# Layer 0's h made one group ahead of the projections that read it, in a two-layer graph attention kernel

## The reference

```python
# layer 0
h = relu(layernorm(x))
m   = h @ map_w.T + map_b                       # 8 heads of 64
cos = (m / |m|) @ (m / |m|).T  per head, masked ; cos_adj = cos > 0.1
q, k = m @ q_w.T + q_b, m @ k_w.T + k_b
p   = softmax(where(mask, NEG, q @ k.T / 8)) * keep
A   = cos_adj * p
out = relu((A @ (h @ gcn_map_w.T + gcn_map_b)) @ gcn_W.T / (A.sum(-1) + 1))
x = x + out
# layer 1: h = relu(layernorm(x)); 4-head masked attention on h, projected out; x = x + that
```

## Time and profile before

| | |
|---|---|
| median of 3 runs | 2962.06 us (2953.75 to 2968.97) |
| the profiled execution, its own time | 2967.72 us |
| its span, first to last instruction | 2965.3 us |
| TensorE busy | 2723.9 us, 92% of the span |
| VectorE, ScalarE, POOL busy | 2011.9, 1743.9, 1578.7 us |
| mean granted TensorE clock | 0.97 of full speed |
| DMA engines' busy share | queue q1, 56.7% |

### The profile page before, as it was taken

One profiled execution on the slowest core, in us unless ns is written; L12 is line 12 of the kernel. 1 busy time (PEld: TensorE's weight loads), 2 busy tenths in 40 slices (PEclk: granted clock), 3 DMA queues, 4 the chain that ended last, 5 costly groups with the idle time before them and its releaser, 6 DMA issues. The chain is left out here.

```text
span 2965.3 us, 63358 instructions
## 1 busy us (share of the span) xinstructions
PE 2723.9 (92%) x20883; PEld 1479.9 (50%) x20886; DVE 2011.9 (68%) x6356; ACT 1743.9 (59%) x4891; POOL 1578.7 (53%) x4146
## 2 busy tenths in 40 slices
PE   5999999999989999999999999957999999999997
PEld 3444444444544454444444444434556555555554
DVE  4476777676767676777677667656666766676764
ACT  3466666565656565656656566535666666666663
POOL 1466566556655665566556646523554455545541
PEclk8999999999999999999999999968999999999998
DMA  4265655655565656565656556555665656556652
GB/s 126 55 123 122 128 132 123 131 123 129 123 137 123 133 122 128 125 132 124 132 133 125 121 126 138 107 133 119 157 155 146 160 146 158 149 144 159 152 137 64
DMA packets 826070, 385.37 MB, mean 130 GB/s; under 512 B 722832, under 2 KB 724368, under 8 KB 825744
## 3 DMA queue, kind: packets, MB, share of 16 engines
q1 hardware_dynamic: 825744, 381.33, 56.7%
HBM read 146.32 MB, written 67.11 MB: 72 GB/s over the span
## 5 line engine op out<-in xcount | busy, mean ns | idle before, releaser
L510 ACT ACTIVATE probs<-probs,negmax 128x128 f32<-128x128 f32 x1024 | 398.2, 390 | 553.1 <-DVE negmax L119 553.1
L161 PE MATMUL ps_pj<-wm_hi,hT 128*128 128x512 f16 x1024 | 340.4, 395 | 99.9 <-DMA hT<-h 84.4
L427 POOL TENSOR_TENSOR o_sb<-o_sb,xres 128x512 f32<-128x512 f32 x128 | 162.9, 1272 | 460.6 <-DVE o_sb L650 457.3
L119 DVE CUSTOM_DVE_ANT_0 probs<-ps_sc,mask 128x128 f32<-128x128 f32 x1024 | 236.5, 286 | 197.5 <-PE ps_sc L835 196.1
L161 PE MATMUL ps_pj<-wv_hi,hT 128*128 128x512 f16 x1024 | 326.8, 380 | 0.0
L161 PE MATMUL ps_pj<-hT,wq_hi 128*128 128x512 f16 x1024 | 310.4, 385 | 0.0
L161 PE MATMUL ps_pj<-hT,wk_hi 128*128 128x512 f16 x1024 | 305.8, 380 | 0.0
L1103 ACT ACTIVATE l_probs<-l_probs,l_negmax 128x128 f32<-128x128 f32 x512 | 199.1, 390 | 150.2 <-DVE l_negmax L119 150.2
L1072 POOL TENSOR_TENSOR l_xres<-l_xres,l_bo_rows 128x512 f32<-128x512 f32 x128 | 171.0, 1336 | 158.4 <-DMA l_xres<-x_scratch 158.3
L632 DVE SCALAR_TENSOR_TENSOR c<-cprobs,c 128x512 f16<-128x512 f32 x256 | 205.2, 802 | 36.9 <-ACT c L517 28.2
L161 PEld LDWEIGHTS ps_pj<-wm_hi,hT 128*128 128x128 f16 x1024 | 103.0, 101 | 225.8 <-DMA hT<-h 95.2
(11 more groups left out here) (192 smaller groups left out, 7037.6 us busy)
## 6 DMA issues: line engine op xcount, KB each, us to landing
xg<-in_x SPq DMA_DIRECT2D x32, 1024.0 KB, 5.8
xres<-in_x SPq DMA_DIRECT2D x128, 256.0 KB, 2.9
x_scratch<-o_sb SPq DMA_DIRECT2D x128, 256.0 KB, 2.1
xg<-x_scratch SPq DMA_DIRECT2D x128, 256.0 KB, 3.0
l_xres<-x_scratch SPq DMA_DIRECT2D x128, 256.0 KB, 3.4
out<-l_o_sb SPq DMA_DIRECT2D x128, 256.0 KB, 3.7
cpT<-c SPq DMA_TRANSPOSE x256, 3.3
mask_u<-in_adj SPq DMA_DIRECT2D x32, 64.0 KB, 5.7
```

The costliest lines, as they stand in the source:

```text
L119: last = nc.vector.tensor_tensor_reduce(masked[:, i], scores[:, i // 2, (i % 2) * P:(i % 2 + 1) * P], mask, -1.0, FLOAT_MAX, ALU.add, ALU. ...
L161: last = pe.matmul(out, a(kt), b(kt), start=(n == 0), stop=(n == 3 * kts - 1))
L427: nc.gpsimd.tensor_tensor(o_sb[:, j % 2], o_sb[:, j % 2], xres[:, j % 2], ALU.add).then_inc(res_done, 1)
L510: last = nc.scalar.activation(probs[:, i], probs[:, i], ACT.Exp, bias=negmax[:, u % 2, i:i + 1], scale=-1.0, accum_out=zsum[:, u % 4, hh:h ...
```

## The change

h's factors, relu, split and transposes of group t + 2 are made during group(t), one group before the projections read them. In group(t) the order is now: POOL `factors(t+2)` at u = 0; ScalarE `relu` and `h_high` (t+2, u-2) at u = 2 to 5, behind n_high; VectorE `h_low(t+2, u-3)` at u = 3 to 6, ahead of n_low and p_low; SyncE `transpose_h(t+2, u-3)` at u = 3 to 6, between transpose_n and transpose_p. xg is loaded one group further ahead: `load_graphs(t+3)` stands at u = 6 behind transpose_p, and all four `stats(t+3, j)` at u = 7 between row_max and epilogue. `convert_mask` goes from u = 5 to u = 6. In front of the first group all of group 1's h is made and group 2's x is loaded.

```diff
+            def load_graphs(g):
+                sp.wait_ge(relu_done, count(QUAD * g))
+                sp.dma_start(xg[:], xt[g]).then_inc(x_loaded, 16)
...
             for j in range(QUAD):
                 transpose_n(0, j)
-                if j == 2:
-                    transpose_h(1, 0)
+                transpose_h(1, j)
+            load_graphs(2)
...  SyncE, group(t)
                     if proj and 3 <= u < 3 + QUAD:
                         transpose_n(t + 1, u - 3)
-                    hg, hj = (t + 1 + (u + 1) // 8, (u + 1) % 8)
-                    if hj < QUAD and hg < GROUPS:
-                        transpose_h(hg, hj)
+                    if ahead and 3 <= u < 3 + QUAD:
+                        transpose_h(t + 2, u - 3)
                     transpose_p(8 * t + u)
+                    if t + 3 < GROUPS and u == 6:
+                        load_graphs(t + 3)
                     if ahead and u == 1:
-                        sp.wait_ge(relu_done, count(QUAD * (t + 2)))
-                        sp.dma_start(xg[:], xt[t + 2]).then_inc(x_loaded, 16)
                         sp.wait_ge(mask_ready, count(t + 1))
...  POOL, group(t)
-                    if proj and u == 5:
+                    if ahead and u == 0:
+                        factors(t + 2, 0, QUAD)
+                    if proj and u == 6:
                         convert_mask(t + 1)
-                    if ahead and u == 6:
-                        factors(t + 2, 0, QUAD)
...  ScalarE, group(t)
-                    hg, hj = (t + 1 + (u + 2) // 8, (u + 2) % 8)
-                    if hj < QUAD and hg < GROUPS:
-                        relu(hg, hj)
-                        h_high(hg, hj)
+                    if ahead and 2 <= u < 2 + QUAD:
+                        relu(t + 2, u - 2)
+                        h_high(t + 2, u - 2)
...  VectorE, group(t)
-                    hg, hj = (t + 1 + (u + 1) // 8, (u + 1) % 8)
-                    if hj < QUAD and hg < GROUPS:
-                        h_low(hg, hj)
+                    if ahead and 3 <= u < 3 + QUAD:
+                        h_low(t + 2, u - 3)
...
-                    if ahead and u in (4, 5):
-                        stats(t + 2, 2 * (u - 4))
-                        stats(t + 2, 2 * (u - 4) + 1)
+                    if t == 0 and u == 0:
+                        for j in range(QUAD):
+                            stats(2, j)
+                    if t + 3 < GROUPS and u == 7:
+                        for j in range(QUAD):
+                            stats(t + 3, j)
```

More of the change, by code:

```diff
@@ L543, in _ @@
             for b in range(KT):
-                if b >= 2:
-                    relu(1, b - 2)
-                    h_high(1, b - 2)
+                relu(1, b)
+                h_high(1, b)
                 q_copy(0, b)
@@ L552, in group @@
             def group(t):
-                proj = t + 1 < GROUPS
+                proj, ahead = t + 1 < GROUPS, t + 2 < GROUPS
                 for u in range(8):
@@ L731, in _ @@
             for b in range(KT):
-                if b == 2:
-                    h_low(1, 0)
+                h_low(1, b)
                 n_low(0, b)
```

## The result

The changed kernel takes 3031.41 us (median of 4, 3026.8 to 3039.37) against 2958.51 for the kernel before in the same comparison: ratio 1.0244, 95% interval 1.0206 to 1.0283. It is slower, by 73 us; 3016 was forecast, with a range of 2940 to 3055. The profiled execution took 3028.03 us (span 3026.2).

What follows compares the result with a forecast made beforehand. POOL's norms chain through SyncE's store and transposes to cpT(5) was taken to bound the cycle. 57.03 + 1.33 + 1.0 + 1.0 + 0.25 gave 60.6 us a cycle against 58.82, so 3016 us, range 2940 to 3055.

Steps and rivals of the forecast that it cites:

- signs of being wrong: Prediction wrong if xg lands before VectorE gets there, norms are not longer, or TensorE doesn't wait at u=6.
- hT one group early: TensorE's waits for hT at u=0 to 3 go; worth 0.37 us on the chain, leaving 57.03.
- SyncE's order, +1.33: On SyncE, transpose_h ahead of transpose_p at u=5 issues cpT(5) later, adding 1.33 us a cycle.
- h_low beside POOL's norms, +1.0: VectorE's h_low subtractions, moved to u=3 to 6, slow POOL's small norm instructions, adding 1.0 us a cycle.
- net two more: Each step's POOL norms meet net two more VectorE subtractions, 0.4 to 0.5 us each.
- the stated bounds: Limits for h_low's cost to POOL's norms: 0 if subtractions fall into gaps, 1.5 us for three full ones.
- The statistics at u=7, +1.0: VectorE, doing four stats at u=7, waits for xg loaded at u=6; POOL's norms start 1.0 us later.
- Jitter and clock, +0.25: Jittering landings and clock lost after the longer stall at u=6 add 0.25 us a cycle.
- the port: VectorE and POOL lock each other out of SBUF; h_low's move therefore costs POOL's norms 1.0 us a cycle.
- Rival 1: xg's load is in time, so VectorE doesn't stand at u=7: cycle 58.9 us, 2962 us; chance 0.14.
- Rival 2: hT waits are real gain, with h_low under 0.9 us and xg in time: 57.9 us, about 2934; chance 0.18.
- Rival 3: xg lands 1 us later, clock falls, n_high holds ScalarE: cycle 62.2 us, 3061 us; chance 0.10.

Runs made afterwards that it cites:

- experiment 3: Kernel before, with SyncE's store and residual load of a step moved behind its transposes: 2934.84 us, ratio 0.9922.
- experiment 11: Kernel of experiment 10 with xg in quarters, one ahead of each step's transposes at u=3 to 6: 2791.06 us, ratio 0.9429.
- experiment 1: Kernel after, with transpose_h moved behind transpose_p on SyncE: 3047.95 us, ratio 1.0305.
- experiment 2: Kernel after, with xg loaded in four quarters, one behind the transposes of each step u=3 to 6: 2951.55 us, ratio 0.9989.
- experiment 9: Kernel of experiment 8 with transpose_h moved behind transpose_p: 2949.26 us, ratio 0.9966.
- experiment 7: Kernel after, with the whole load of xg ahead of the three transposes of u=6: 2980.93 us, ratio 1.0073.
- experiment 8: Kernel of experiment 2 with each quarter of xg ahead of its step's transposes: 2978.4 us, ratio 1.007.
- experiment 4: Kernel after, with transpose_h behind transpose_p, xg in quarters placed last, and store and residual load behind the transposes: 2876.56 us, ratio 0.9731.
- experiment 5: Kernel after, with xg in quarters behind the transposes and transpose_h behind transpose_p: 2943.62 us, ratio 0.9959.
- experiment 6: Kernel of experiment 4 with each quarter of xg ahead of its step's transposes: 2788.59 us, ratio 0.9428.
- experiment 10: Kernel after, with store and residual load behind the step's three transposes: 2980.75 us, ratio 1.0075.

## Why the prediction was right, point by point

The sign and the size came out, the sign by the mechanism that the prediction said decides it (xg's load at u=6), the size partly by luck: a cost that hardly came and others that came larger cancelled. One of its own signs of being wrong showed: POOL's norms did not get longer.

**hT one group early.** Right: no wait for hT is left, and with SyncE's order as it is here that is no gain in itself. Experiment 3 shows the exchange of the two waits from the other side. It becomes a gain when the store no longer stands ahead of the transposes: without h one group early that kernel takes 2934.84 us (experiment 3), with it and the quarters 2791.06 (experiment 11). The quarters in the kernel of 3 were not run, so how much of the 144 us is h's alone stays open.

**SyncE's order, +1.33.** The size is right: cpT(5) left 3.79 us behind the residual instead of 2.39, +1.40. That it adds to the cycle is not: experiment 1 took it out and nothing came back. In the kernel after it is not what closes the cycle. The waits for cpT were foreseen as 3 to 4 us a cycle at u=6; there they are 2.13, in 25 of 28 cycles, and the total of 3.97 is made up by the 1.83 at u=4, which the prediction had seen and rightly priced at nothing.

**h_low beside POOL's norms, +1.0.** Wrong. POOL's chain took 30.61 us, against 30.5 in clean cycles and a mean of 31.05 before, which had 0.55 us of idle time in it (0.02 after). Where the three subtractions stand back to back on VectorE, three of POOL's small instructions run long; here in the cycle shown, VectorE and then POOL:

```profile
1126.75 0.68 DVE L590 TENSOR_TENSOR h<-h 128x512 f16<-128x512 f32 x1
1127.35 0.69 DVE L612 SCALAR_TENSOR_TENSOR n<-m_sb,n 128x512 f16<-128x512 f32 x1
1128.19 0.73 DVE L633 SCALAR_TENSOR_TENSOR c<-cprobs,c 128x512 f16<-128x512 f32 x1 [0.16 <-ACT c L520]
```

```profile
1126.80 0.69 POOL L77 TENSOR_TENSOR norm_st<-norm_st 128x8 f32<-128x8 f32 x1
1127.57 0.53 POOL L78 TENSOR_TENSOR norm_st<-norm_st,consts 128x8 f32<-128x8 f32 x1
...
1128.45 0.53 POOL L76 TENSOR_TENSOR norm_st<-norm_st 128x8 f32<-128x8 f32 x1
```

Counted between 200 and 1800 us, 218 small instructions of POOL ran long before (8.0 a cycle) and 262 after (10.0). So the "net two more" of the step is right, and its price is not: they lose 0.36 us each over the usual 0.20 instead of 0.43, and the sum of what they lose is nearly the same, 93 us in both, or 3.4 us a cycle before and 3.6 after. The traces also show why three in a row cost less each. Every one of the 218 and 262 long instructions ends 0.05 to 0.10 us, nearly always 0.06, behind the end of such a subtraction (as 1127.49 behind 1127.43 above), and none of the usual length lies inside one: a POOL instruction loses what is left of the subtraction when it comes, not the whole of it. Before, it came 0.13 us after the subtraction's start in the mean, and after, with three in a row, 0.20. The 10 long ones of a chain lost 3.55 us against 3.40 for 8 before: +0.15, near the lower end of the stated bounds. The price is not fixed: in experiments 1, 2 and 9, with h_low in the same place, the 10 lost 3.8 to 3.9 us and the chain took 30.9 to 31.0, so some 0.45. The rule of the Trainium skill (SBUF — State Buffer, section Who interferes with whom), that the port pair shared by VectorE and GpSimd is an exclusive lock, agrees with these ends of instructions; the 1.4 that the prediction worked out from it does not, since it took two whole subtractions where only their remainders are lost.

**The statistics at u=7, +1.0.** The mechanism is right in each of its parts: VectorE's stand of 2.71 us, in all 29 cycles that load xg (2 to 3, some 29 times, were forecast; two more stands lie ahead of them), m_copy late, TensorE held at u=1, POOL late. Its size was +1.49 against before's mean, or +1.68 against 13.64. The term mis-sized is the load: forecast 5.4 us behind the issue of cpT(5) and 5.7 to land, so 14.7 us from the residual to the first statistics; measured 9.38 to the issue and 6.68 from there to use, 16.06. From the end of the statistics to POOL's norm it is 11.12, where the prediction's figures give 14.64 - 3.6 = 11.04. The landing of 1 MB behind six transposes takes 1 us longer, and the issue is 0.2 further behind that of cpT(5) than forecast. Of the excess of 0.68 over the forecast 14.64, 0.4 is xg's arrival against u0 (u0 + 0.93 instead of 0.55; u0 is later too), 0.24 the statistics (3.29 instead of 3.05), and the rest what follows them. The 14.64 is near the median of 14.73; the mean is drawn up by the 8 late cycles. The prediction's 4.9 us for this load, an estimate by the Trainium skill (DMA: Bandwidth & Descriptors, Specifications and the anatomy of one DMA), lies below every landing after as well (5.7 at the least); the fixed cost in it is one that the page gives for DMAs issued from GpSimd, and these are issued by SyncE.

**Jitter and clock, +0.25.** Too small. Taken with the rest of the cycle, from the matmul of cpT(5) to the next u0 it is 7.80 in the mean, against 7.18 + 0.25, and 8.70 in the cycle shown, where TensorE has just stood 2.95 us. That stretch, with the columns of the earlier trace rows:

```profile
1155.50:1164.20 8.70, 8.69 (x68) 4.30 (x69) 3.35 (x14) 3.15 (x11) 1.26 (x1) 0.80 0.97 244
```

TensorE is busy throughout at a clock of 0.80, the mix of 2.4 and 1.2 GHz of the earlier trace rows. Over the 1600 us the mean clock fell from 0.99 to 0.97.

**The sum.** Against the forecast of 60.61 the terms are +0.68 (to the norms), -0.94 (POOL), +0.17 (SyncE), +0.15 (landing), +0.37 (rest): 61.04. The port's 0.94 too much was outweighed by 1.37 too little in the other four. 0.43 a cycle in 29 cycles is 12 us; the profiled execution came 6 us over the 3022 that were named for it, and the median 15 over 3016. What the prediction did not see is that it had written down two loops and added their terms. It closed the cycle with cpT(5) and let xg's delay enter as a term; in fact xg's arrival hangs on the same POOL chain through nearly three transposes more, and runs in a loop of its own:

```
2nd residual to xg's issue          9.38
issue to first statistics           6.68
four statistics                     3.29
to POOL's first norm               11.12
POOL's chain                       30.61
                                   61.08
```

Both sums give the cycle, as any walk round it does, and stands do not tell them apart: VectorE stands for xg in every cycle, but TensorE stands for cpT(3) in every cycle too, and for cpT(5) in 25 of 28. The experiments that change one loop each decide it: shortening the way to cpT(5) gains nothing (1), shortening the arrival of xg gives back 80 us (2). Without the stand POOL starts some 12.8 us after u0 (experiments 7 to 9), and the loop through cpT(5) sums to about 58.5 us, no longer than the 58.84 of before. So the sign came from xg's loop alone: with xg in time the change is worth nothing either way (experiment 2). The advice drawn from the sum (put transpose_h behind transpose_p) would have been wrong for the kernel after.

**The rivals.** Rival 1 (xg in time, 58.9 us, 2962 us): the chip has it in experiment 2, 58.77 us and 2951.55 us. Its price was right, though with 1.0 for the port where 0.45 was paid; its condition does not hold in the change. Rival 2 (57.9 us, 2934 us) had its first condition met, the port costing under 0.9, but not its second. Experiment 2 meets both and still takes 58.77, so its price was 0.9 us a cycle too low. Rival 3 (everything late, 3061 us) had in it the late landing of xg behind six transposes and more clock loss, and 3031 lies between it and the forecast.

## What to carry to other kernels

Where a cycle has several loops of nearly one length through one in-order queue, write down each loop with its sum before pricing a move: the term of a loop that doesn't close the cycle is worth nothing. A stand of an engine in every cycle makes a loop a candidate and no more, since here two engines stood in every cycle; an experiment that shortens one loop alone decides. On an in-order DMA queue a blocking store ahead of unrelated issues ties these to the engine that it waits for, and transposes ahead of a load tie it to whoever makes their data. Here the store went behind the step's transposes and the load, in pieces, ahead of them, and these two edits turned +2.4% into -5.7%. A whole load ahead of the transposes with the store late was not run, so whether the pieces are needed stays open; with the store in its old place the whole load ahead made the queue's next transposes slow (experiment 7).

## What the runs showed of the hardware

- A load of 1 MB behind six DMA transposes landed in 6.5 us (median) instead of 5.7. In four pieces of 256 KB the loads landed in 3.1 us (median) behind a step's transposes (experiments 2, 4 and 5), in 3.2 ahead of them with the store in its old place (8 and 9), and in 2.9 with the store late (6 and 11).
- With 1 MB issued two issues ahead, a DMA transpose held SyncE's queue 3.8 to 4.7 us instead of 1.3, in 27 of 28 cycles (experiment 7).
- A load of 256 KB ahead of a step's transposes cost cpT(5) 0.8 us of issue and 0.3 of landing (experiments 2 and 8).
- POOL's small instructions (0.20 us) beside VectorE's two-input subtractions (0.69 us) never lay inside one: those that ran long, 218 before and 262 after, all ended 0.05 to 0.10 us behind the subtraction's end. What they lost is the remainder of the subtraction, 0.43 us in the mean before and 0.36 after.
- TensorE idle 5.85 us a cycle came with a mean clock of 0.97 (after), 4.43 with 0.96 (experiment 10), 4.32 with 0.99 (before), and 0.09 with 0.99 (experiment 6): the idle time alone does not order the clocks.
